# The head of the next sequence's Mamba block moved into the FFN, its convolution split over ACT and Pool, dt spread in larger packets

## The chip, the cores and the metric

One core of one Trainium2 chip runs the whole kernel in one launch. The metric is the device time of an execution in microseconds, the median over the timed runs. The five engines are called PE (TensorE), DVE (VectorE), ACT (ScalarE), Pool (GpSimd) and SP (SyncE, which here only issues DMAs).

## The reference

The reference is a two-layer decoder over 16 independent sequences (batch) of 256 tokens with 256 features, all in float32. Six sublayers follow each other, each as `x = layernorm(x + sublayer(x))`:

```
xz = x @ W_in (256 -> 1024);  xin, z = split(xz)
xc = silu(causal_depthwise_conv(xin, 4 taps) + conv_b)          # 512 channels
dt_low, Bm, Cm = split(xc @ W_xproj, [64, 16, 16])
dt = softplus(dt_low @ W_dt + b_dt)
h_t = exp(dt_t * A) * h_(t-1) + dt_t * B_t * xc_t               # 16 states a channel, 256 steps
y = (sum_n h*C + xc*Dp) * silu(z);  out = y @ W_out
```

That is the first, Mamba. Then come a latent cross-attention (16 heads of 16, 64 chosen keys a query), an FFN with quantised activations and ternary weights (256 -> 1024 -> 256, GELU, two inner norms), a self-attention (16 heads of 16), a cross-attention (16 heads of 64) and a mixture of eight experts with six chosen, plus a shared one. Mamba, latent attention and FFN are layer 0; the other three are layer 1.

## The kernel before

Each engine has one program of its own, and semaphores order them. A sequence is a unit of work: its 256 tokens are handled as 2 x 128 rows, or as 256 columns when channels lie on partitions. Inside, the work is two streams. Stream x is `mamba`, `latent` and `ffn` of a sequence; stream y is `self_attention`, `cross_attention` and `moe` of the sequence before. On each engine, each stream is a generator that yields between pieces, and `merged` (L58) interleaves the two by a written-out string: `ORDER` (L41) says for each engine how many pieces stream x is ahead at the start and then the turns of one period ("x9 y3 x1 ..."), repeated for every sequence. An engine works strictly in that order; a piece that waits holds all behind it. The state of a sequence's x goes from x to y through `X.x_ready`, whose third count comes from `ffn_end` (L1546): the last residual add and norm.

`mamba` of a sequence, before: PE projects 8 tiles of 128 channels (`projected`, L494) into four PSUM banks. ACT copies the first half of each bank into `xin` (L980) and writes the last tap's product with the bias into `conv` (L983); DVE adds the other three taps with twelve fused steps (L1383). ACT applies SiLU (L999, L1003). PE makes the low-rank dt (L516) and C rows (L519), the full dt in two halves (L543), the B rows (L549). DVE adds dt's bias (L1395), ACT computes the parts of the softplus (L1015 to L1018), DVE puts them together and multiplies by xc (L1406 to L1413). In between, a table of how often each key was chosen is counted by one-hot matmuls (L471), turned (L480) and made into a mask.

The state recurrence then runs in `UNITS` = 32 units. A unit has 8 channels x 16 states on the 128 partitions and 2 x 256 columns. Its dt rows and dt*x rows must be repeated 16 times over the partitions: SP stores them to a buffer in DRAM, `rows_of_dt` (L323), and reads them back with a repeating pattern, `spread_rows` (L325), one DMA of 256 KB for each unit and each of dt and dt*x, into four slots each. Per unit ACT writes exp(dt*A) to PSUM (L1028), DVE multiplies dt*x by B (L1432) and runs the scan along the columns (L1449), Pool multiplies by C (L1227), and PE sums over states, four units at a time (L561). ACT may be at most two units ahead of the scan; the spread of unit k waits for the decay, or the product, of unit k - 4. `gate` (L1418) and the output projection (L569) end the block.

`region_x`, one SBUF tensor of 11,792 words a partition, is carved into overlapping tiles that stages use in turn. xc, zs, conv, xin and the softplus tiles share its words with the FFN's tiles (`fh`, `qb`, `qT`), so the head of a `mamba` can begin to write only when the FFN before it is through.

In `ffn`, DVE's steps (norm, quantisation, L1527, one-hots L1351) alternate with small bf16 matmuls. In `moe`, PE makes gate and up groups of two tiles (L864), spreads the routing weights (L870) and does the down product (L925); ACT applies SiLU (L1189), DVE multiplies twice (L1646, L1650). ACT holds one set of functions at a time; `table` (L950) loads another when a piece needs it (L952).

Of the kernel before, what the change touches and what calls it, by code (L numbers as in the profile page):

```python
# [21 lines left out]
SLOTS = 4  # L22
# [70 lines left out]
X_STEPS = 70  # L93
END_STEPS = 5
DIGIT_STEPS = 8
Y_STEPS = 38
A_STEPS = 7
# [22 lines left out]
def build(nc, dram, out):  # L120

    ctx = ExitStack()
    with ctx:
# [45 lines left out]
        RX, RY = 11792, 9216  # L169
# [22 lines left out]
        PAD = T + TAPS - 1  # L192
        xc, zs, yT, csb = in_x(0, (M, T)), in_x(1024, (M, T)), in_x(2048, (M, T)), in_x(3072, (T,))
        conv = yT
        dtr = in_x(11536, (T,))
        xin = in_x(3328, (M, PAD))
        sp_l = in_x(3328, (M, T))
        sp_x, sp_e, sp_u = in_x(4364, (M, T)), in_x(5388, (M, T)), in_x(6412, (M, T))
# [3 lines left out]
        oh_hi, oh_lo = in_x(4608, (P, 32), BF16), in_x(10508, (P, 16), BF16)  # L202
        cnt = in_x(6656, (P, 16), BF16)
# [16 lines left out]
        scratch = nc.dram_tensor("rows_of_dt", (2, 2, P, M * T), F32)  # L220
# [16 lines left out]
        dt_exp = sem("dt_exp")  # L237
        digit_step, end_step = sem("digit_step"), sem("end_step")
        xz, xin_sb, conv_done, silu_x, silu_z = sem("xz"), sem("xin_sb"), sem("conv_done"), sem("silu_x"), sem("silu_z")
# [72 lines left out]
        att1 = Attention("self", 4, False, 1, VP1, nm1, in_y, 7424)  # L312
        att2 = Attention("cross", 4)

        block = ctx.enter_context(nc.Block())


        @block.sync
# [1477 lines left out]
```

## Time and profile before

| | |
|---|---|
| median of 3 timed runs | 3942.16 us (3936.2 to 3948.75) |
| the profiled execution | 3951.12 us, its span 3949.3 us |
| busy: PE, DVE, ACT, Pool | 3210.4 (81%), 3004.6 (76%), 1953.3 (49%), 650.5 (16%) |
| DMA | 470.84 MB, mean 119 GB/s |
| chain that ended last | PE 41%, DVE 34%, ACT 9%, issue 8%, DMA 6% |
| granted TensorE clock, mean | 0.933 |

A span is the time from the first to the last instruction of one profiled execution. Busy time of an engine counts its instructions' durations, overlaps once. The "chain that ended last" is followed back from the last instruction through whatever released each step. The program repeats one period for each sequence, so the tables below cut one steady period (1424.0 to 1657.8 us from the start) into stretches.

### The profile page before, as it was taken

How to read it: one execution, taken by the hardware profiler on the slowest of the kernel's cores; microseconds unless marked ns; L12 is line 12 of the kernel's file. 1: busy time of each engine (PE TensorE's matmuls, PEld its weight loads, DVE VectorE, ACT ScalarE, POOL GpSimd, SP SyncE). 2: the span in 40 equal slices, each digit the busy share in tenths (PEclk: the TensorE clock that was granted, in tenths of full speed). 3: DMA queues.
4: the chain of work that ended last, by engine and by line, in shares of the span. 5: the costliest groups of instructions: out<-in, count | busy, mean ns of one | idle time of the engine just before them, and what ended most of it. 6: DMA issues, size and time to landing. Idle time of an engine off the chain costs nothing.

```text
span 3949.3 us, 57618 instructions
## 1 busy us (share of the span) xinstructions
PE 3210.4 (81%) x21250; PEld 2199.1 (56%) x21250; DVE 3004.6 (76%) x6496; ACT 1953.3 (49%) x4513; POOL 650.5 (16%) x516
## 2 busy tenths in 40 slices
PE   2468988788797888978888897988879888887877
PEld 1245656556464655646556564655646565564655
DVE  5678796877878688796868879687887868778632
ACT  2336455564545546455554645555464554645422
POOL 0303030120303012040210304021030301204000
PEclk8679999999999989999999999989999998999987
DMA  6526171532716235181523517153361614427100
GB/s 213 131 56 174 50 197 63 157 119 89 203 50 184 77 123 153 54 238 49 155 95 116 171 50 225 52 159 99 96 196 50 197 63 146 130 74 215 55 31 16
DMA packets 205833, 470.84 MB, mean 119 GB/s; under 512 B 23856, under 2 KB 43952, under 8 KB 190832
## 3 DMA queue, kind: packets, MB, share of 16 engines
q1 hardware_dynamic: 205552, 467.17, 39.2%
q8 instruction: 167, 2.74, 0.3%
q14 instruction: 114, 0.93, 0.1%
HBM read 446.11 MB, written 20.97 MB: 118 GB/s over the span
## 4 chain that ended last, share of the span: by engine, by line
PE 41%; DVE 34%; ACT 9%; issue 8%; DMA 6%; SPq 1%; POOL 0%; DVEq 0%; ACTq 0%
DVE region_x L1449 7%; PE ps L864 6%; DMA region_x<-rows_of_dt 5%; DVE region_x L1432 5%; PE ps L633 4%; PE ps L824 3%; PE ps L810 3%; PE ps L497 3%; ACT region_y L1148 3%; PE ps L845 3%; PE ps L614 2%; DVE nm L1486 2%; PE ps L645 2%; DVE x_stats L1284 2%; PE ps L569 2%
## 5 line engine op out<-in xcount | busy, mean ns | idle before, releaser
L1227 POOL TENSOR_TENSOR region_x<-region_x 128x512 f32<-128x512 f32 x512 | 650.3, 1270 | 2982.6 <-DVE region_x L1449 2982.6
L1028 ACT ACTIVATE ps<-region_x,aneg 128x255 f32<-128x255 f32 x1024 | 443.1, 470 | 446.2 <-DVE region_x L1449 431.3
L1449 DVE TENSOR_TENSOR_SCAN region_x<-ps,region_x 128x512 f32<-128x512 f32 x512 | 622.9, 1217 | 16.0 <-ACT ps L1028 15.1
L1432 DVE TENSOR_TENSOR region_x<-region_x,ps 128x512 f32<-128x512 f32 x512 | 343.1, 671 | 49.2 <-DMA region_x<-rows_of_dt 46.2
L864 PE MATMUL ps<-xTy,wide 128*128 128x256 f32 x1280 | 307.1, 395 | 0.0
L1148 ACT ACTIVATE region_y<-ps,rmax 128x256 f32<-128x256 f32 x512 | 235.7, 500 | 140.9 <-DVE rmax L1591 140.9
L1499 DVE SCALAR_TENSOR_TENSOR region_x<-region_x,cntk 128x512 f32<-128x512 f32 x256 | 167.0, 689 | 156.2 <-ACT region_x L1066 156.2
L864 PEld LDWEIGHTS ps<-xTy,wide 128*128 128x128 f32 x1280 | 244.5, 196 | 42.3 <-issue 10.1
L561 PE MATMUL ps<-region_x,sely 128*32 128x512 f32 x1024 | 157.5, 691 | 121.6 <-POOL region_x L1227 121.3
L614 PE MATMUL ps<-region_y 64*128 64x256 f32 x1024 | 176.9, 485 | 91.5 <-DVE VP L1572 37.4
L633 PE MATMUL ps<-region_y 64*128 64x256 f32 x1024 | 173.1, 464 | 95.9 <-ACT region_y L1066 49.5
L1591 DVE TENSOR_REDUCE rmax<-ps 128x4 f32<-128x1024 f32 x128 | 153.2, 1218 | 111.2 <-PE ps L791 109.7
L1482 DVE CUSTOM_DVE_ANT_0 region_x<-ps,mask 128x256 f32<-128x256 f32 x512 | 184.7, 420 | 40.1 <-issue 40.1
L925 PE MATMUL ps<-down,region_y 128*128 128x256 f32 x640 | 183.4, 454 | 37.2 <-DVE region_y L1650 37.2
L1164 ACT ACTIVATE region_y<-ps 128x512 f32<-128x512 f32 x256 | 140.6, 597 | 142.1 <-PE ps L813 142.1
L633 PEld LDWEIGHTS ps<-region_y 64*128 64x128 f32 x1024 | 103.0, 217 | 190.9 <-ACT region_y L1066 131.3
L614 PEld LDWEIGHTS ps<-region_y 64*128 64x128 f32 x1024 | 113.4, 236 | 155.0 <-DVE nm L1486 60.6
L1066 ACT ACTIVATE region_x<-ps 128x512 f32<-128x512 f32 x256 | 141.2, 605 | 86.6 <-PE ps L633 86.6
L925 PEld LDWEIGHTS ps<-down,region_y 128*128 128x128 f32 x640 | 146.0, 233 | 64.9 <-issue 38.7
L791 PE MATMUL ps<-region_y 64*128 64x256 f32 x1024 | 138.7, 406 | 41.7 <-DVE region_y L1586 24.6
L1066 ACT ACTIVATE region_y<-ps 128x512 f32<-128x512 f32 x256 | 138.3, 593 | 52.9 <-PE ps L633 52.0
L810 PE MATMUL ps<-region_y 64*128 64x256 f32 x1024 | 156.5, 397 | 8.9 <-ACT shiftT L1157 7.6
(246 smaller groups left out, 6491.9 us busy)
## 6 DMA issues: line engine op xcount, KB each, us to landing
region_x<-rows_of_dt SPq DMA_DIRECT2D x1024, 256.0 KB, 5.3
wide<-in_wgate SPq DMA_DIRECT2D x16, 1280.0 KB, 8.4
wide<-in_wup SPq DMA_DIRECT2D x16, 1280.0 KB, 11.0
down<-in_wmoe SPq DMA_DIRECT2D x16, 1280.0 KB, 5.6
wide<-in_wq SPq DMA_DIRECT2D x16, 1024.0 KB, 4.8
wide<-in_wk SPq DMA_DIRECT2D x16, 1024.0 KB, 6.9
wide<-in_wv SPq DMA_DIRECT2D x16, 1024.0 KB, 8.9
down<-in_wo SPq DMA_DIRECT2D x16, 1024.0 KB, 7.8
```

Source lines behind the costliest of these rows:

```text
L614: last = mm(ps[:, b + j, qt * T:(qt + 1) * T], a.QT[r, t, qt * P:(qt + 1) * P], a.KT[u % 2][r, t, :], start=True, stop=True)
L633: last = mm(ps[:, a.sT_bank(n + j), kt * T:(kt + 1) * T], a.KT[e][r, t, kt * P:(kt + 1) * P], a.QT[r, t, :], start=True, stop=True)
L810: mm(ps[:, b, kt * T:(kt + 1) * T], KT2[r, t, kt * P:(kt + 1) * P], QT2[r, t, :], start=True, stop=False)
L864: last = mm(bank(b)[:, j, :], w[:, k, f * P:(f + 1) * P], xTy[:, k, :], start=(k == 0), stop=(k == KD - 1))
L925: last = mm(bank(7)[:, tt, :], mhT[:, f, tt * P:(tt + 1) * P], wmoe[:, f, :], start=(n == 0), stop=(n == KM - 1))
L1028: last = f(ps[:, 1 + 2 * (k % 2), m * T + 1:(m + 1) * T], dt_rep[k % SLOTS][:, m, 1:T], ACT.Exp, scale=aneg[:, k, m:m + 1])
L1066: f(a.PT[:, n % 8].rearrange("p k q -> p (k q)"), ps[:, a.sT_bank(n), :], ACT.Exp).then_inc(a.probs, 1)
L1148: last = f(junk2[:, 4 * (u % 2) + 2 * qt + g], ps[:, a.pair_bank(u) + g, qt * T:(qt + 1) * T], ACT.Exp, bias=rmax[:, qt, g, u:u + 1], accu ...
L1227: nc.gpsimd.tensor_tensor(hbuf[k % HSLOTS], hbuf[k % HSLOTS], csb.unsqueeze(1).to_broadcast([P, 2, T]), ALU.mult).then_inc(hc_ready, 1)
L1432: tt_(hbuf[k % HSLOTS], dtx_rep[k % SLOTS], ps[:, 2, 0:T].unsqueeze(1).to_broadcast([P, 2, T]), ALU.mult).then_inc(dbx, 1)
L1449: nc.vector.tensor_tensor_scan(flat(hbuf[k % HSLOTS]), ps[:, 1 + 2 * (k % 2), :], flat(hbuf[k % HSLOTS]), 0.0, ALU.mult, ALU.add).then_inc ...
L1482: last = nc.vector.tensor_tensor_reduce(a.junk[:, 4 * (u % 2) + 2 * qt + j], ps[:, b + j, qt * T:(qt + 1) * T], mask[:, qt, :], -1.0, HUGE ...
```

## The change

Six things change together.

1. The head of the next sequence's Mamba (in-projection, convolution, gates, low rank, C rows, dt, B rows, turned counts) is issued inside `ffn` of the present one. Only the joining of dt's second half, the masks and the counts by key stay in `mamba`. The head of sequence 0 runs ahead of both streams.
2. `region_x` grows by 5,376 words, in which xc, zs, conv, the taps, C and the softplus tiles lie apart from the FFN's.
3. The convolution: ACT makes all four products from PSUM (three of them into `taps`, shifted), Pool adds them, three serial sums for each half.
4. dt's bias is added by ACT instead of DVE.
5. The store to DRAM lays two groups of channels next to each other, and one DMA spreads two units: 512 KB, 4,096 bytes a partition and packet, three slots of two units.
6. All four turn strings are new; also some PSUM banks in the FFN, and a smaller scratch for software DMA. With the new turns the y stream of a sequence starts eight units into the next sequence's scan, and the second part of `moe` lies at the scan's beginning.

The core of the diff:

```
-SLOTS = 4
+COUPLES = 3
...
-        RX, RY = 11792, 9216
+        EARLY = 11792
+        RX, RY = EARLY + 5376, 9216
...
-        dt_rep = [in_x(7436 + 512 * s, (2, T)) for s in range(SLOTS)]
-        dtx_rep = [in_x(9484 + 512 * s, (2, T)) for s in range(SLOTS)]
+        dt_rep = [in_x(at_word, (2, 2, T)) for at_word in (7436, 8460, 0)]
+        dtx_rep = [in_x(at_word, (2, 2, T)) for at_word in (9484, 10508, 0 + 1024)]
...
-        scratch = nc.dram_tensor("rows_of_dt", (2, 2, P, M * T), F32)
+        scratch = nc.dram_tensor("rows_of_dt", (2, 2, 2, 32, 4, 2 * T), F32)
...
+            def spread_rows(i, what, d, dst):
+                rows = scratch[i % 2, what, d // 8, 8 * (d % 8 // 2):8 * (d % 8 // 2) + 8, 2 * (d % 2):2 * (d % 2) + 2]
+                return sp.dma_start(dst.rearrange("p k m t -> p (k m t)"),
+                                    rows.rearrange("r j f -> r (j f)").unsqueeze(0).to_broadcast([NS, 8, 4 * T]))
...
+                for d in range(UNITS // 2):
+                    slot = couple(i, d)[0]
...
+                    if d >= COUPLES:
+                        sp.wait_ge(decay_ready, at(i, UNITS, 2 * (d - COUPLES) + 2))
+                    spread_rows(i, 0, d, dt_rep[slot]).then_inc(rep_dt[slot], 16)
...
# PE, in ffn
+                        projected(i + 1, n)            # two pieces, at the start
...
+                    projected(i + 1, 2)                # after the FFN's first product
+                    projected(i + 1, 3)
+                    yield from low_rank(i + 1)         # low rank, C rows, dt
+                    pe.wait_ge(silu_z, i + 2)
                     yield from counted(i + 1, 0, 2)
...
+                    yield from b_rows(i + 1)           # after the FFN's second product
+                    yield from counted(i + 1, 2, 4)
+                    yield from counts_turned(i + 1)
...
+            def conv_products(i, half):
+                act.wait_ge(xz, at(i, 4, half + 1))
+                if half:
+                    act.wait_ge(conv_sum, at(i, 6, 3))
+                for j in range(2):
+                    m = 2 * half + j
+                    f(conv[:, m, :], bank(half)[:, j, :], ACT.Identity, bias=W["convb"][:, m:m + 1],
+                      scale=W["convw"][:, m, TAPS - 1:TAPS])
+                    for k in range(TAPS - 1):
+                        late = TAPS - 1 - k
+                        last = f(taps[k][:, j, late:T], bank(half)[:, j, 0:T - late], ACT.Copy,
+                                 scale=W["convw"][:, m, k:k + 1])
+                last.then_inc(taps_sb, 1)
...
+            def conv_sums(i):                          # Pool, after the 32 products of a sequence
+                for half in range(2):
+                    pool.wait_ge(taps_sb, at(i, 2, half + 1))
+                    part = conv[:, 2 * half:2 * half + 2, :]
+                    for k in range(TAPS - 1):
+                        if k:
+                            pool.wait_ge(conv_sum, at(i, 6, 3 * half + k))
+                        nc.gpsimd.tensor_tensor(part, part, taps[k], ALU.add).then_inc(conv_sum, 1)
...
# DVE, mamba
-                            ins = stt(conv[:, m, :], xin[:, m, k:k + T], W["convw"][:, m, k:k + 1], conv[:, m, :],
-                                      ALU.mult, ALU.add)
...
+                yield from dt_half(dt_steps, i, 1)
```

The order of the pieces around the handover, as the new strings give it (x7 is stream x of sequence 7, y5 stream y of sequence 5, and so on):

```
ACT: ... x6 cnt3 | x7 rstd5 | y5 gate0 | x7 decay0 | y5 gate1 wT | x7 decay1 | y5 gate2 | x7 decay2 | y5 gate3 | x7 decay3 | y5 gate4 | x7 decay4..7 ...
SP:  x6 rows, choices+xT | x7 store0 | y5 ctx | x7 store0' | y5 wide_moe | x7 spreads 0, 1, store1, spread 2 | y5 wmoe | x7 spreads 3, 4 | y5 wide_cross | x7 spread 5 | y5 wo2, out | x7 spread 6 ...
```

## Rows read from the trace of the kernel before

**Rows 1.** By stretch: us, busy of PE, PEld, DVE, ACT, Pool; clock, DMA, GB/s.

```profile
1424.00:1657.80 233.80, 198.82 (x1336) 136.95 (x1332) 186.66 (x405) 121.90 (x283) 40.65 (x32) 0.95 0.40 123
1424.00:1452.50 28.50, 26.13 (x128) 20.00 (x124) 20.16 (x52) 16.96 (x32) 0.00 (x0) 0.94 0.27 83
1452.50:1536.50 84.00, 64.29 (x387) 37.19 (x387) 79.42 (x106) 44.12 (x105) 40.65 (x32) 0.92 0.82 236
1536.50:1603.30 66.80, 62.52 (x490) 43.82 (x489) 37.27 (x126) 40.04 (x112) 0.00 (x0) 1.00 0.07 28
1603.30:1657.80 54.50, 45.88 (x335) 35.94 (x333) 49.80 (x123) 20.79 (x35) 0.00 (x0) 0.94 0.24 89
```

**Rows 2.** The head in two parts, then two DVE groups of it (count, busy us, mean ns).

```profile
1424.00:1438.50 14.50, 14.50 (x80) 10.66 (x76) 10.50 (x33) 10.84 (x20) 0.00 (x0) 1.00 0.00 1
1438.50:1452.50 14.00, 11.63 (x51) 9.34 (x50) 9.66 (x19) 6.12 (x12) 0.00 (x0) 0.88 0.55 167
...
L1383 DVE SCALAR_TENSOR_TENSOR region_x<-region_x,convw 128x256 f32<-128x256 f32 x12 | 5.3, 483 | 0.8 <-ACT region_x L983 0.6
L1395 DVE TENSOR_SCALAR region_x<-ps,bdt 128x256 f32<-128x256 f32 x4 | 1.7, 479 | 2.1 <-PE ps L543 2.1
```

**Rows 3.** Instruction groups of the scan stretch, DVE.

```profile
L1449 DVE TENSOR_TENSOR_SCAN region_x<-ps,region_x 128x512 f32<-128x512 f32 x32 | 39.0, 1217 | 0.9 <-ACT ps L1028 0.8
L1432 DVE TENSOR_TENSOR region_x<-region_x,ps 128x512 f32<-128x512 f32 x32 | 21.4, 671 | 1.9 <-DMA region_x<-rows_of_dt 1.7
```

**Rows 4.** Instruction groups of the FFN stretch, PE and DVE.

```profile
L864 PE MATMUL ps<-xTy,wide 128*128 128x256 f32 x80 | 18.5, 385 | 0.0
L925 PE MATMUL ps<-down,region_y 128*128 128x256 f32 x40 | 11.6, 458 | 2.3 <-DVE region_y L1650 2.3
...
L1646 DVE TENSOR_TENSOR region_y<-region_y,ps 128x512 f32<-128x512 f32 x4 | 2.7, 684 | 0.2 <-PE ps L864 0.2
```

**Rows 5.** Instruction groups of the scan stretch that the new order takes out.

```profile
L765 PE MATMUL ps<-wide,ctxT 128*128 128x512 f32 x16 | 7.1, 599 | 0.0
L779 PE MATMUL ps<-xTy,wide 128*128 128x256 f32 x32 | 7.4, 386 | 0.7 <-ACT xTy L969 0.7
L791 PE MATMUL ps<-region_y 64*128 64x256 f32 x24 | 3.1, 393 | 2.3 <-DVE region_y L1586 1.5 <-ACT region_y L1148 0.9
...
L1586 DVE TENSOR_SCALAR region_y<-ps 128x512 f32<-128x512 f32 x4 | 2.6, 681 | 0.0
L1591 DVE TENSOR_REDUCE rmax<-ps 128x4 f32<-128x1024 f32 x2 | 2.4, 1223 | 0.1
```

**Rows 6.** ACT's table loads of the period, and one in order of time.

```profile
L952 ACT ACT_TABLE_LOAD x7 | 9.0, 1283 | 0.1
...
1425.94 1.28 ACT L952 ACT_TABLE_LOAD   x1
1427.23 0.60 ACT L980 ACTIVATE region_x<-ps 128x512 f32<-128x512 f32 x1
```

**Rows 7.** Order of time, Pool and DVE (start us, us, what).

```profile
1510.89 1.26 POOL L1227 TENSOR_TENSOR region_x<-region_x 128x512 f32<-128x512 f32 x1 [0.43 <-DVE region_x L1449]
...
1510.90 1.28 DVE L1297 SCALAR_TENSOR_TENSOR y_nt<-y_nt,y_rstd 128x2 f32<-128x2 f32 x1
```

**Rows 8.** Spreads, then expert weights, by stretch; and one row of the DMA issues.

```profile
1480.00:1490.00 10.00, 8.22 (x80) 3.75 (x72) 7.87 (x10) 8.85 (x21) 5.86 (x5) 1.00 1.02 258
1530.50:1541.00 10.50, 8.63 (x56) 5.95 (x56) 7.35 (x10) 5.55 (x24) 2.47 (x2) 1.00 0.99 407
...
wide<-in_wup SPq DMA_DIRECT2D x16, 1280.0 KB, 11.0
```

**Rows 9.** Order of time, PE: first transposes of three y streams.

```profile
269.88 0.66 PE L459 MATMUL ps<-ident,xh 128*128 128x128 f32 x4
...
3539.45 0.66 PE L459 MATMUL ps<-ident,xh 128*128 128x128 f32 x4
...
3759.80 1.09 PE L459 MATMUL ps<-ident,xh 128*128 128x128 f32 x4 [4.13 <-DVE xh L1303]
```

More of the change, by code:

```diff
@@ new lines, in projected, with low_rank @@
+            def projected(i, n):
+                for m in (2 * n, 2 * n + 1):
+                    for k in range(KD):
+                        last = mm(bank(n)[:, m % 2, :], W["win"][:, k, m * P:(m + 1) * P],
+                                  xTx[:, k, :], start=(k == 0), stop=(k == KD - 1))
+                last.then_inc(xz, 1)
+            def low_rank(i):
+                yield
+                for k in range(M):
+                    pe.wait_ge(silu_x, at(i, 2, k // 2 + 1))
+                    last = mm(ps[0:RANK, 0, 0:T], W["wxd"][:, k, :], xc[:, k, :], start=(k == 0), stop=(k == M - 1))
+                last.then_inc(xdbl, 1)
+                yield
+                for k in range(M):
+                    last = mm(ps[:, 1, 0:T], W["wc"][:, k, :], xc[:, k, :], start=(k == 0), stop=(k == M - 1))
+                last.then_inc(xdbl, 1)
@@ L679, in ffn @@
             def ffn(i):
+                more = i + 1 < B
+                for n in range(2):
+                    yield
+                    if more:
+                        if n == 0:
+                            pe.wait_ge(xT_loaded, at(i + 1, 16, 16))
+                            pe.wait_ge(X.sum_read, at(i, 3, 2))
+                        projected(i + 1, n)
                 psb = ps[:, 3, :].bitcast(BF16).rearrange("p (a b) -> p a b", b=T)
@@ L931, in all_first @@
                     pass
+                pe.wait_ge(xT_loaded, 16)
+                for n in range(3):
+                    projected(0, n)
+                pe.wait_ge(cnt_sb, 4)
+                projected(0, 3)
+                for piece in (low_rank, b_rows, counts_turned):
+                    for _ in piece(0):
+                        pass
                 for i in range(B):
@@ L1199, in all_first @@
                     count_copy(0, r)
+                for half in range(2):
+                    conv_products(0, half)
+                gates(0)
+                for half in range(2):
+                    conv_half(0, half)
+                dt_rank(0)
+                c_copy(0)
+                for half in range(2):
+                    softplus_parts(0, half)
                 before = None
@@ L1222, in _ @@
         def _(pool):
+            def conv_sums(i):
+                for half in range(2):
+                    pool.wait_ge(taps_sb, at(i, 2, half + 1))
[4 more added lines that the diff above has]
+                        nc.gpsimd.tensor_tensor(part, part, taps[k], ALU.add).then_inc(conv_sum, 1)
+            conv_sums(0)
             for i in range(B):
@@ L1389, in mamba @@
-                yield
-                next(before, None)
-                for half in range(2):
-                    yield
-                    v.wait_ge(dt_ps, at(i, 2, half + 1))
-                    for m in (2 * half, 2 * half + 1):
-                        last = ts(sp_x[:, m, :], bank(half)[:, m % 2, :], W["bdt"][:, m:m + 1], None, ALU.add)
-                    last.then_inc(dt_x, 1)
+                next(before, None)
+                yield from dt_half(dt_steps, i, 1)
+                dt_steps.close()
@@ L1454, in mamba @@
                 gate(1)
+                for k in range(TAPS - 1):
+                    nc.vector.memset(taps[k][:, :, 0:TAPS - 1 - k], 0.0)
                 v.wait_ge(x_loaded, at(i, 16, 16))
@@ L1538, in ffn @@
                 yield from quantised(i, c, fh, FF, 3)
+                if i + 1 < B:
+                    yield from dt_half(next_steps, i + 1, 0)
+                else:
+                    yield from [None] * 2
                 for r in (2, 3):
@@ L1664, in all_first @@
                 before = iter(())
+                steps = Chain(v, dt_step, 0, DT_STEPS)
+                for _ in dt_half(steps, 0, 0):
+                    pass
                 for i in range(B):
                     c = Chain(v, vx_step, i, X_STEPS)
-                    yield from mamba(i, c, before)
+                    yield from mamba(i, c, before, steps)
                     if i == 0:
@@ L1670, in all_first @@
                     yield from latent(i, c)
-                    yield from ffn(i, c)
+                    steps = Chain(v, dt_step, i + 1, DT_STEPS)
+                    yield from ffn(i, c, steps)
                     c.close()
```

325 lines of the change are left out of this document (147 added, 178 removed), and 17 rows, old and new, of the table ORDER.

## The prediction

> **What bounds the kernel now.** I read the busy shares by stretch first, then the instruction groups of each stretch, then the waits and the DMA issues. Two streams run interleaved: x (Mamba, latent attention, FFN of one sequence) and y (self-attention, cross-attention, experts of the sequence before). One steady period, from one x stream's FFN end to the next, is the first row of [rows 1]: 233.8 us, PE busy 198.8, DVE 186.7, ACT 121.9. Neither big engine fills it; each stretch has its own limit.
>
> - Head, 28.5 us: PE 26.1. Its first 14.5 us (in-projection to turned counts) are PE without a gap [rows 2]; the scan can't start before it ends.
> - Scan, 84.0 us: DVE 79.4, PE only 64.3.
> - Latent and cross scores, 66.8 us: PE 62.5.
> - FFN beside the experts, 54.5 us: DVE 49.8, PE 45.9.
>
> The limits add up to 26.1 + 79.4 + 62.5 + 49.8 = 217.8, so 16.0 us a period are stalls and handovers. What is wasted is PE under the scan, 84.0 - 64.3 = 19.7 us, because there DVE alone sets the pace: each of 32 units costs a scan of 1217 ns and a product of 671 ns [rows 3].
>
> **The change, part by part, for one period.**
>
> Taken off DVE: twelve convolution steps, 5.3 us, and four bias adds, 1.7 us [rows 2]: 7.0 us. DVE's total becomes 186.7 - 7.0 = 179.7.
>
> PE's total stays 198.8: the same matmuls, moved. The head's 14.5 us go between the latent attention's end and the FFN's end, where the previous order had the experts. In exchange the whole second part of the experts and the self-attention's projections come under the scan. I walked the new turn strings, piece by piece, to see what lies beside what:
>
> - Into the scan stretch, PE: projections and turns of the self-attention, the head's second part, 11.6 [rows 2]; six of the ten gate or up groups, 0.6 x 18.5 = 11.1; the experts' down product, 11.6; the weights' spreading, an estimate of 1.5 (eight matmuls at no more than the down product's 11.6 / 40 would be 2.3) [rows 4]. Together 35.8.
> - Out of it, PE: cross values 7.1, cross queries 7.4, first scores 3.1, and one key group, 1.85 like a gate group [rows 4, 5]: 19.4.
> - PE there: 64.3 + 35.8 - 19.4 = 80.7. DVE there: 79.4, plus eight expert products of 0.68 (four stand in [rows 4], four more cost the same) = 5.4, plus the experts' norm, an estimate of 3.1 (one wide add of 0.68, four steps on 256 columns at 0.48 as in [rows 2], and 0.5 of tiny ones), plus the self queries, four such steps, 1.9, minus cross queries 2.6 and two maxima 2.4 [rows 5]: 84.8.
> - The rest of the period: PE 198.8 - 80.7 = 118.1; DVE 179.7 - 84.8 = 94.9.
>
> The limits are now 84.8 (DVE) and 118.1 (PE), sum 202.9 against 217.8. I keep the 16.0 us of stalls, since the dependency chains inside latent attention, FFN and self-attention are untouched, and add 5 for what is new:
>
> *ACT.* It gets sixteen products on 256 columns where it had two copies and four scaled steps, and the four bias adds: fourteen more, at most 0.6 each like the wide copy of [rows 6], 0.4 in a row, so +6 us. It also alternates: the new order runs gate 0, decay 0, gate 1, decay 1 and so on to gate 4, and each needs another table set. Seven loads of 1283 ns a period [rows 6] become about fourteen, +9 us. ACT has 112 us idle, so the sum costs nothing there; but in five units the chain gate, decay, next gate is 0.6 + 1.0 + 2 x 1.28 = 4.2 us long (the two decays at the same rate as the copy), beside PE's 2 x 1.85 = 3.7 for an expert pair. Lower bound 0, upper bound 5 x (4.2 - 1.9) = 11.5 us, if those units wait for nothing else. I take 3, near zero, because PE sets the pace of that stage anyway.
>
> A page says more. The Trainium skill, page "ScalarE: Activation LUTs", section "What ACT_TABLE_LOAD costs", gives each switch a drain of about the same length again, 2.66 us in all. Here the copy behind a load starts at 1427.23, 1.29 us after the load's start [rows 6], so the trace disagrees; by the page the seven extra loads would cost 19 us of ACT instead of 9, and the exposed part would double, a period of about 227.
>
> *Pool.* Six sums of 128x512, serial in threes; the same form of instruction takes 1.27 us, so 7.6 us in the FFN stretch, where Pool had been idle. The first product half waits for nothing, the second for Pool's first three sums, since the tap buffers are shared; both have some 15 us before the low-rank product needs them, so this latency is hidden. What isn't: at 1510.90 a DVE step on two columns took 1.28 us, as long as the Pool product of 512 columns that started 0.01 us before it [rows 7]. Bounds: 0 if DVE's neighbours read PSUM (as scans and products do, which run beside Pool unharmed), 7.6 if each sum holds DVE once. I take 2.
>
> That observation has a name: the Trainium skill, "SBUF — State Buffer", section "SBUF: two separate sides", calls the pair of ports that DVE and GpSimd share an exclusive lock, held for a whole instruction when DVE has two SBUF inputs. By that rule, which the row bears out, the FFN's two-input steps would pay in full; it is the first rival below.
>
> *DMA.* Spreads move the same bytes in half as many packets. With 2,048-byte packets the engines are saturated at 258 GB/s; loading expert weights they reach 407 [rows 8]. The new rate lies between these. At best the 4.6 us go that DVE idles under the scan [rows 1]; at worst a spread of twice the size lands later than the lead allows, which is now about five units of 1.9 us where it was four: from -4.6 to about +2. I take 0. The weight loads are the third rival.
>
> *Late things.* Once the head is gone, the next late item before the scan is the second half of dt (DVE about 3.1 us) and the masks; both lie beside expert matmuls.
>
> Period: 202.9 + 16.0 + 5 = 223.9, that is -9.9.
>
> **The whole run.** y streams start at 269.9 (first), 3539.5 (15th) and 3759.8 (16th) [rows 9]: 14 periods of 233.5, a last one of 220.3 without a next sequence, and 189.5 to the end. After: the first y stream must wait for the x stream's FFN with the head inside, and for eight units of scan. I put +19 on it (16 for the units at two microseconds each, 9 for Pool's serial sums and the next dt, less the 6 or so of head that now hides in the lone FFN), so 289. The last period drops the head (14.5) and the table switching: 223.9 - 20 = 203.9. Sum: 289 + 14 x 223.9 + 203.9 + 189.5 = 3817. The profiled execution took 3951.1 for a span of 3949.3, and the median of the timed runs is 3942.2, 9 below it: 3817 + 2 - 9 = 3810.
>
> **The rivals.** One microsecond a period is 15 in the run.
>
> 1. *The port between Pool and DVE costs in full.* 7.6 instead of 2: 3810 + 15 x 5.6 = 3894. For: the row above, and that the sums fall beside the FFN's norms, which read two SBUF tensors. Against: DVE isn't the limit there (94.9 of some 129). Chance 0.14.
> 2. *The long PE stretch fills badly.* PE was busy 45.9 of 54.5 in the FFN stretch, 84%; if that share holds for all the rest, 118.1 / 0.84 = 140.6 instead of about 129, less 3 that the scan stretch would keep of its stalls: +8.5 a period, 3937. For: FFN is a serial chain on DVE. Against: cross scores now lie beside it, and with such filler PE reached 94%. Chance 0.12, half of it no change.
> 3. *Slower: the SP queue.* The loads of the expert gates and ups now stand behind the first dt store, and those of the down product and the next cross weights between spreads. At 407 GB/s these 2.56, 1.28 and 3.07 MB take 6.4 + 3.2 + 7.7 = 17.3 us, formerly issued long before use; the second of the expert loads landed 11.0 us after its issue [rows 8]. Spreads behind them in the queue come late, DVE waits. All exposed: 3810 + 15 x 17.3 = 4070. It decides once more than 8.8 of the 17.3 are exposed. For: SP blocks on each load's own wait. Against: by my walk some 10 us of PE and DVE work (two count blocks, the state rows, the residual norm, the router) stand between that issue and the first gate product, so 3 us are exposed there at most. Chance 0.12.
> 4. *Better.* The stalls shrink too (DVE's 4.6 us under the scan go, and with them some of PE's time at a lower granted clock, 0.92 there against 1.00 after it [rows 1]): -7 a period, 3705. Chance 0.13.
>
> **How the numbers follow.** The forecast (3750 to 3875) has 0.49. No change means within 0.3%, 12 us, about what a measurement of this kernel can tell. Faster: 0.49 + 0.14 + 0.13 + half of rival 2 = 0.82, less 0.02 for the forecast's own tail; one of these goes to the same, 0.06 + 0.01 = 0.07, one to slower, 0.12 + 0.01 = 0.13. The range leaves out rival 3, half of rival 2 and the tail of rival 4: 3710 to 3935.
>
> **What would show it.** Right: a steady period near 224; no gap-free PE head before the scan; PE above 85% under the scan; conv steps gone from DVE and Pool at 48.3 us a period; fourteen table loads a period. Wrong: DVE idle in the first scan units on "DMA region_x<-rows_of_dt" or PE idle before the first gate group on weights (rival 3); DVE rows of the FFN above their old means (rival 1); PE below 88% from latent attention to FFN end (rival 2).

## The result: slower, by 7.9%

The changed kernel takes 4259.3 us (median of 4 runs, 4251.3 to 4261.2), the kernel before 3945.5 (4 runs): ratio 1.079, 95% interval 1.076 to 1.082. The forecast was 3810 us, with a range up to 3935. The profiled execution has a span of 4249.5 us.

The page of the kernel after, its engines and the rows that answer to [rows 6, 8] (the last three lines are DMA issues: count, KB each, median us to landing):

```profile
PE 3276.5 (77%) x21234; PEld 2233.4 (53%) x21250; DVE 2970.2 (70%) x6275; ACT 2141.2 (50%) x4802; POOL 775.0 (18%) x612
DMA packets 131337, 470.81 MB, mean 111 GB/s; under 512 B 14896, under 2 KB 34992, under 8 KB 116336
...
L968 ACT ACT_TABLE_LOAD x209 | 268.1, 1283 | 4.4 <-PEq L1849 0.7
...
region_x<-rows_of_dt SPq DMA_DIRECT2D x512, 512.0 KB, 8.6
...
wide<-in_wup SPq DMA_DIRECT2D x16, 1280.0 KB, 17.1
down<-in_wmoe SPq DMA_DIRECT2D x16, 1280.0 KB, 15.9
```

The work is what was forecast: the steps of the convolution have left DVE, Pool has six sums more a period, 14 table loads stand in a period. What is different is when DMAs land: the load of the experts' up weights (wup) takes 17.1 us where it took 11.0 [rows 8].

The y streams, in order of time on PE, as in [rows 9]:

```profile
310.23 0.69 PE L466 MATMUL ps<-ident,xh 128*128 128x128 f32 x2
...
3833.92 0.55 PE L466 MATMUL ps<-ident,xh 128*128 128x128 f32 x3
...
4059.66 0.55 PE L466 MATMUL ps<-ident,xh 128*128 128x128 f32 x3 [0.78 <-DVE xh L1384]
```

A steady period is (3833.92 - 310.23) / 14 = 251.7 us; it was 233.5, and 223.9 was forecast. The other terms: first y start 310.2 for 289, last period 225.7 for 203.9, 189.8 to the end for 189.5. So of the 432 us by which the sum (3817) missed the span, 14 x 27.8 = 389 lie in the steady periods. This section and the next look for them there; "period" always means this quotient of a profiled execution.

One period, from a first scan to the next, in three parts cut at places that both orders have: first to last scan; on to the end of latent attention; on to the next first scan. Columns as in [rows 1]. The kernel before, cut this way:

```profile
1216.15:1295.45 79.30, 60.42 (x356) 35.08 (x358) 73.35 (x94) 40.60 (x92) 39.38 (x31) 0.92 0.84 221
1295.45:1371.19 75.74, 68.75 (x530) 47.36 (x526) 43.85 (x142) 43.06 (x123) 1.26 (x1) 1.00 0.17 64
1371.19:1455.63 84.44, 72.49 (x447) 56.16 (x446) 69.61 (x169) 38.35 (x67) 0.00 (x0) 0.91 0.24 83
```

The kernel after; behind it the stretch around the scan's start in which DMA is full, and 10 us of it in which only spreads are in flight:

```profile
1291.82:1384.06 92.24, 68.27 (x403) 43.26 (x402) 78.09 (x104) 49.61 (x102) 39.23 (x31) 0.92 0.79 205
1384.06:1466.73 82.67, 71.29 (x458) 50.13 (x458) 45.59 (x148) 39.04 (x116) 1.46 (x2) 0.99 0.06 21
1466.73:1544.17 77.44, 62.50 (x472) 44.71 (x472) 60.99 (x140) 46.10 (x84) 7.78 (x6) 0.89 0.35 107
...
1279.00:1350.00 71.00, 57.50 (x290) 40.77 (x288) 51.55 (x78) 34.89 (x62) 20.36 (x16) 0.92 0.88 245
...
1336.00:1346.00 10.00, 6.29 (x36) 4.40 (x38) 9.89 (x13) 2.62 (x6) 3.81 (x3) 0.83 1.03 243
```

The period shown of the kernel before is its longest, 239.5 us. Over the 13 steady periods of each, the three parts are on the mean 77.1, 75.8 and 80.8 us before and 92.5, 81.5 and 77.5 us after, so the differences are read from these.

Read three things here. The last part got only 3 us shorter on the mean: DVE (61.0) and PE (62.5) both sit idle for 15 to 16 us of it. The scan got 15 us longer, with only 4.5 more of DVE work (means of 73.1 and 77.6). And DMA is as good as full from 13 us before the scan to 58 us into it (0.88), while it is nearly idle, 21 GB/s, for the 83 us after. Spreads alone fill the engines at 243 GB/s with packets of 4,096 bytes, where it was 258 with 2,048 [rows 8], in a window that also holds a load of the next x: the larger packets bought no rate.

The waits of the kernel after (total us, times, longest); for the first row the kernel before had 46.2:

```profile
DVE region_x L1485 <- DMA region_x<-rows_of_dt: 145.3, 86, 8.2
DVE cntq L1433 <- PE ps L487: 107.0, 14, 9.0
...
PE ps L872 <- DMA wide<-in_wup: 102.0, 14, 8.0
...
DVE xh L1384 <- PE ps L933: 51.6, 16, 9.1
```

And the place of the third row in one period, PE in order of time:

```profile
1278.33 6.30 PE L872 MATMUL ps<-xTy,wide 128*128 128x256 f32 x16 [7.42 <-DMA wide<-in_wup]
1284.56 1.17 PE L487 MATMUL ps<-identb,region_x 32*128 32x32 bf16 x16
1285.66 3.72 PE L872 MATMUL ps<-xTy,wide 128*128 128x256 f32 x16
```

The first expert group waits 7.4 us for its weights and then runs at a lower clock, 6.30 us for what takes 3.72 right after (the granted clock is 0.72 on the mean of 1273 to 1291.8, so for somewhat over half of that time it is at the lower of its two levels, 1.2 of 2.4 GHz). The counts that DVE needs (L487) stand behind it on PE, so DVE waits as well: the second row of the waits.

### The profile page after: what moved, and what is told of

Read it like the earlier page. It is cut to its first block, busy times and chain, and to the rows that moved or that the text cites. A ratio compares the mean times of both kernels' runs of the same rounds, so it can differ in the third digit from the quotient of the medians.

```text
span 4249.5 us, 57375 instructions
## 1 busy us (share of the span) xinstructions
PE 3276.5 (77%) x21234; PEld 2233.4 (53%) x21250; DVE 2970.2 (70%) x6275; ACT 2141.2 (50%) x4802; POOL 775.0 (18%) x612
## 4 chain that ended last, share of the span: by engine, by line
PE 37%; DVE 23%; ACT 15%; DMA 15%; issue 7%; SPq 2%; POOL 1%; DVEq 0%; POOLq 0%; ACTq 0%
DMA region_x<-rows_of_dt 6%; DMA wide<-in_wup 6%; PE ps L601 4%; PE ps L872 4%; DVE region_x L1502 4%; PE ps L933 3%; ACT region_y L1195 3%; PE ps L620 3%; DMA out_x<-xh 3%; PE ps L787 2%; PE ps L773 2%; DVE region_x L1485 2%; ACT ps L1053 2%; PE ps L502 2%; DVE nm L1541 2%
## 5 line engine op out<-in xcount | busy, mean ns | idle before, releaser
L1294 POOL TENSOR_TENSOR region_x<-region_x 128x512 f32<-128x512 f32 x512 | 650.7, 1272 | 1737.3 <-DVE region_x L1502 1737.3
L872 PE MATMUL ps<-xTy,wide 128*128 128x256 f32 x1280 | 330.1, 416 | 102.0 <-DMA wide<-in_wup 102.0
L1287 POOL TENSOR_TENSOR region_x<-region_x 128x512 f32<-128x512 f32 x96 | 124.1, 1293 | 1390.4 <-ACT region_x L1002 1385.4
L872 PEld LDWEIGHTS ps<-xTy,wide 128*128 128x128 f32 x1280 | 260.3, 209 | 152.4 <-DMA wide<-in_wup 103.4
L601 PE MATMUL ps<-region_y 64*128 64x256 f32 x1024 | 179.9, 494 | 118.0 <-DVE VP L1631 65.4
L620 PE MATMUL ps<-region_y 64*128 64x256 f32 x1024 | 185.1, 491 | 98.8 <-ACT region_y L1091 59.6
L1195 ACT ACTIVATE region_y<-ps,rmax 128x256 f32<-128x256 f32 x512 | 237.9, 496 | 16.6 <-DVE rmax L1650 14.5
L601 PEld LDWEIGHTS ps<-region_y 64*128 64x128 f32 x1024 | 116.3, 240 | 197.2 <-DVE VP L1631 86.5
L620 PEld LDWEIGHTS ps<-region_y 64*128 64x128 f32 x1024 | 109.5, 231 | 186.8 <-ACT region_y L1091 134.5
L799 PE MATMUL ps<-region_y 64*128 64x256 f32 x1024 | 143.4, 399 | 75.7 <-ACT region_y L1195 61.7
L1211 ACT ACTIVATE region_y<-ps 128x512 f32<-128x512 f32 x256 | 141.6, 594 | 107.1 <-PE ps L821 106.8
L1384 DVE TENSOR_TENSOR xh<-ps,xh 128x512 f32<-128x512 f32 x80 | 55.2, 690 | 199.0 <-PE ps L662 71.0
L818 PE MATMUL ps<-region_y 64*128 64x256 f32 x1024 | 165.7, 415 | 16.9 <-ACT region_y L1211 15.0
## 6 DMA issues: line engine op xcount, KB each, us to landing
wide<-in_wup SPq DMA_DIRECT2D x16, 1280.0 KB, 17.1
wide<-in_wv SPq DMA_DIRECT2D x16, 1024.0 KB, 13.8
```

The costliest lines, as they stand in the source:

```text
L601: last = mm(ps[:, b + j, qt * T:(qt + 1) * T], a.QT[r, t, qt * P:(qt + 1) * P], a.KT[u % 2][r, t, :], start=True, stop=True)
L620: last = mm(ps[:, a.sT_bank(n + j), kt * T:(kt + 1) * T], a.KT[e][r, t, kt * P:(kt + 1) * P], a.QT[r, t, :], start=True, stop=True)
L818: mm(ps[:, b, kt * T:(kt + 1) * T], KT2[r, t, kt * P:(kt + 1) * P], QT2[r, t, :], start=True, stop=False)
L872: last = mm(bank(b)[:, j, :], w[:, k, f * P:(f + 1) * P], xTy[:, k, :], start=(k == 0), stop=(k == KD - 1))
L1195: last = f(junk2[:, 4 * (u % 2) + 2 * qt + g], ps[:, a.pair_bank(u) + g, qt * T:(qt + 1) * T], ACT.Exp, bias=rmax[:, qt, g, u:u + 1], accu ...
L1294: nc.gpsimd.tensor_tensor(hbuf[k % HSLOTS], hbuf[k % HSLOTS], csb.unsqueeze(1).to_broadcast([P, 2, T]), ALU.mult).then_inc(hc_ready, 1)
```

## The experiments

Each ran beside the kernel before on the same chip; from chip to chip the median of the kernel before differs by at most 6 us (3941 to 3947). e4 and e5 leave work out and only show what it costs. The table has the median, the ratio to the kernel before, the period, and DVE's wait for spreads summed over the run.

| run | us | ratio, 95% interval | period | DVE on spreads |
|---|---|---|---|---|
| before | 3945 | 1 | 233.5 | 46 |
| after | 4259 | 1.079 (1.076 to 1.082) | 251.7 | 145 |
| e1_wide_early | 4201 | 1.064 (1.062 to 1.066) | 247.3 | 223 |
| e2_out_late | 4232 | 1.071 (1.069 to 1.074) | 250.5 | 263 |
| e3_small_packets | 4225 | 1.070 (1.068 to 1.072) | 250.1 | 136 |
| e4_pool_tiny | 4140 | 1.049 (1.047 to 1.051) | 243.7 | 268 |
| e5_cross_tiny | 4106 | 1.041 (1.039 to 1.043) | 241.3 | 121 |
| e6_before_cross_late | 4001 | 1.015 (1.013 to 1.018) | 237.1 | 85 |
| e7_fewer_tables | 4184 | 1.062 (1.060 to 1.063) | 247.4 | 129 |
| e8_sums_on_dve | 4181 | 1.060 (1.058 to 1.062) | 246.7 | 224 |
| e9_moe_early | 4148 | 1.053 (1.050 to 1.056) | 243.9 | 147 |
| e10_loads_apart | 4143 | 1.051 (1.048 to 1.054) | 243.5 | 121 |
| e11_loads_last | 4058 | 1.028 (1.026 to 1.030) | 237.9 | 60 |
| e12_all_mended | 4110 | 1.041 (1.038 to 1.043) | 241.9 | 60 |
| e13_sums_dve_only | 4041 | 1.024 (1.021 to 1.026) | 236.8 | 58 |
| e14_small_packets_clean | 4061 | 1.029 (1.026 to 1.033) | 238.4 | 59 |

**First four: which of the suspects, queue order, packets, Pool.**

```
e1   sp order: -"x14 y1 x1 y1 x8 ..."  +"x13 y2 x10 ..."          (ctx, wgate, wup ahead of store 0)
e2   e1, and  -"... x2 y2 x10"  +"... x4 y2 x8"                  (wo2, output store behind couple 6)
```

> SyncE's order alone is changed: the context rows and the two wide expert loads (wgate, wup) are issued before the first dt store instead of behind it. Theory A (the queue order is the loss): the wait of PE for wup at the first gate group (7.3 us, 14 times) goes, and the slow clock after it (the group ran 6.3 instead of 3.7 us), so 7 to 10 us in each of some 15 periods: 4259 becomes 4110 to 4155 us. Theory B (DMA bandwidth is the loss, the order only says who waits): the spreads and stores wait instead, and no more than 3 us per period come back: 4215 us or more. Theory C (Pool sums holding DVE up, and PE's own new stretch, are the loss): within 15 us of 4259.

> As the run before, and the loads of wo2 and the output store are issued behind the spreads of couple 6 instead of ahead of them. Theory A: DVE's three spread waits at units 9 to 13 (3.79, 2.75 and 2.25 us) shrink, and as DVE sets the scan 4 to 8 us per period more come back: 60 to 120 us below the run before. Theory B: the spreads are late because DMA is full, so the waits only move by a couple: less than 30 us below it.

e1 came between the theories. PE's wait for wup is gone from the trace and the last part of the period falls from 77 to 70 us, but DVE's spread waits grow from 145 to 223 us: more than half of what PE gave back was waited for again under the scan. e2 is worse than e1 by 31 us, against theory A: the loads that it moved now stood ahead of other couples. Both say that the queue has no room where these loads stand.

```
e3   one transfer of [128, 2 units] per couple -> two of [128, 1 unit], semaphore counts 32
```

> The kernel after with each spread of a couple as two transfers with packets of 2,048 bytes, as before, in the same order and at the same place in SyncE's queue. Theory A: the packets don't matter, the landing is set by what stands ahead: 4259 with at most 25 us either way (32 more issues per period on SyncE may cost some). Theory D (the larger transfers are late because both units of a couple land together): the first unit lands earlier, DVE's and ACT's waits for rows_of_dt (145 and 70 us) at least halve, and the time falls by 60 us or more.

34 us faster, 9 beyond the bound of theory A and far from the 60 of D; DVE's wait for spreads hardly changed (136), that for wup fell by 12. So the packets' size had some part beside the large loads; through what is not shown, for the two waits make up 21 of the 34 us. e14 below repeats it with these loads moved.

```
e4   e2, and  -tensor_tensor(part, part, taps[k], add)  +tensor_tensor(part[:, :, 0:8], ..., taps[k][:, :, 0:8], add)
```

> As the run with wo2 and the output store late, but the three Pool sums of the convolution work on 8 of the 256 columns only (most of the sums are left out; instructions, waits and order are the same). If GpSimd's hold on the port costs what the lengthened DVE steps show (0.9 to 0.16, 1.98 to 0.91 and so on, 5 to 6 us a period, plus up to 3 us of latency of the sums before silu), the time falls by 60 to 120 us against that run; if DVE isn't what sets the FFN's end (PE is), by less than 25 us.

92 us less than e2 by the medians, about 6 a period. By the profiled executions it is 6.8, but that of e2 is its slowest, 16 us above its median. DVE's steps under a Pool sum in the kernel after:

```profile
1220.65 0.91 DVE L1368 SCALAR_TENSOR_TENSOR x_nt<-x_mv,x_rstd 128x2 f32<-128x2 f32 x1 [1.18 <-ACT x_rstd L981]
...
1221.79 1.12 DVE L1370 SCALAR_TENSOR_TENSOR x_rstd<-x_nt,x_rstd 128x2 f32<-128x2 f32 x1
1222.94 1.98 DVE L1377 SCALAR_TENSOR_TENSOR region_x<-region_x,x_rstd,ln1b 128x256 f32<-128x256 f32 x2
...
1228.04 1.23 DVE L1403 TENSOR_SCALAR region_x<-region_x 128x256 bf16<-128x256 f32 x1
1229.20 0.21 DVE L1409 CAST region_x<-idx 128x128 f32<-128x128 int32 x1
1229.45 1.18 DVE L1410 TENSOR_SCALAR region_x<-region_x 128x128 f32<-128x128 f32 x1
1230.66 1.38 DVE L1411 TENSOR_TENSOR region_x<-region_x 128x128 f32<-128x128 f32 x1
```

and the same steps with the sums cut to 8 columns, then the last part of the period in that run:

```profile
1439.58 0.16 DVE L1368 SCALAR_TENSOR_TENSOR x_nt<-x_mv,x_rstd 128x2 f32<-128x2 f32 x1 [1.18 <-ACT x_rstd L981]
...
1439.97 0.16 DVE L1370 SCALAR_TENSOR_TENSOR x_rstd<-x_nt,x_rstd 128x2 f32<-128x2 f32 x1
1440.16 0.88 DVE L1377 SCALAR_TENSOR_TENSOR region_x<-region_x,x_rstd,ln1b 128x256 f32<-128x256 f32 x2
...
1444.17 0.29 DVE L1403 TENSOR_SCALAR region_x<-region_x 128x256 bf16<-128x256 f32 x1
...
1444.63 0.23 DVE L1410 TENSOR_SCALAR region_x<-region_x 128x128 f32<-128x128 f32 x1
1444.89 0.29 DVE L1411 TENSOR_TENSOR region_x<-region_x 128x128 f32<-128x128 f32 x1
...
1433.44:1496.73 63.29, 59.86 (x473) 43.45 (x472) 55.33 (x139) 45.95 (x84) 2.39 (x6) 0.97 0.24 65
```

The part is 63.3 us long with DVE busy 55.3; in e2 it is 70.1 with 61.1. Six sums of 1.27 us, 7.6 in all, take 5.8 us of DVE. With that gone the part is 6.8 us shorter, so once the weights are there DVE's chain sets its length, though PE is as busy (61.7 us in e2, 59.9 in e4).

**Second four: bytes, the same fault in the old kernel, table loads, the sums' place.**

```
e5   e1, and load_wide_cross() -> load_wide_cross(32)             (32 of 1,024 columns after the first time)
e6   before, sp order: -"x2 y3 x1 y1 x17 y1 x5 ..."  +"x2 y3 x17 y1 x1 y1 x5 ..."
e7   e1, act order: -"y1 x1 y2 x1 y1 x1 y1 x1 y1 x4 y1"  +"y1 x1 y3 x2 y2 x5 y1"
e8   e1, conv_sums() off Pool; the same six adds in DVE's stream, behind the norm and behind the digits
```

> As e1_wide_early, but the three cross-attention weights (3.07 MB a period) are loaded in full only once; later loads bring 32 of 1,024 columns (most of the transfer is left out; issues and waits stay). Theory B, as the first runs have changed it (the queue is full from about 13 us before the first scan to 58 us after it, so weights that the new order reloads beside the spreads cost DVE their transfer time): DVE's 14.0 us of spread waits a period fall to 5 or less, and 9 to 11 us a period come back: 4201 becomes 4035 to 4070. Theory A (the order in the queue alone matters, and DMA has room): less than 3 us a period, 4155 or more.

> The kernel before, with one thing of the change: SyncE issues the cross-attention weights behind the spreads of unit 6's predecessors, so among the spreads, instead of ahead of the first dt store. Theory B: the same loss appears in the old kernel, 3.07 MB at 250 to 400 GB/s = 8 to 12 us a period less 2 to 4 of slack: 3946 becomes 4030 to 4110. Theory A: the weights are needed only after 16 units, the buffers are four units ahead, nothing waits: within 30 us of 3946.

e5 gives 95 us back and halves DVE's spread waits, from 223 to 121: the bytes count, though less than theory B had it, 6.0 us a period for loads of 3.15 MB (the 3.07 MB of the expectations counts the page's KB, which are 1,024 bytes, as 1,000). e6 shows the loss in the old kernel: nothing but the place of the cross weights in SyncE's queue, with their use far off, costs 59 us (3.6 a period). That is less than the 84 to 164 expected and well clear of nothing, and PE never waits for these weights in it. Its one row of the waits, the kernel before with the cross weights among the spreads:

```profile
DVE region_x L1432 <- DMA region_x<-rows_of_dt: 84.8, 86, 5.4
```

The bytes are not all. SyncE issues in its written order, and a wait of its own holds all behind it. Two such waits of the kernel after, one for the experts' down product before wo2 is loaded, one for the output store to land before the next x is loaded:

```profile
SPq L421 <- PE ps L933: 105.1, 15, 9.3
SPq L336 <- DMA out_x<-xh: 92.3, 14, 8.7
```

In the kernel before the first happens once (14.6 us) and the second is not among the waits. e5 shows what such waits can do with the bytes out of the way: SyncE in order of time, and a stretch of the same trace.

```profile
1263.34 1.20 SPq L332 DMA_DIRECT2D region_x<-rows_of_dt  x2
1271.36 0.33 SPq L421 DMA_DIRECT2D down<-in_wo  x1
1275.08 0.40 SPq L424 DMA_DIRECT2D out_x<-xh  x1
1275.54 1.17 SPq L332 DMA_DIRECT2D region_x<-rows_of_dt  x2
...
1268.00:1272.00 4.00, 3.42 (x20) 2.69 (x22) 3.00 (x4) 0.00 (x0) 2.73 (x3) 1.00 0.40 118
```

DMA falls to 0.40 while the next couple isn't issued, and DVE waits 1.54 us for spreads at 1283.54. By couple, counted from 0, DVE's waits over the run fall from 87 us in e1 to 1 in e5 at couple 5, the first behind the cross weights, but only from 34 to 23 and from 32 to 31 at couples 6 and 7, which stand behind wo2, the store and the next x. In the kernel after DMA stays full (1.02 and 1.03) through the same two waits of SyncE, so there its waits and the bytes can't be told apart; no run takes SyncE's waits out alone.

> As e1_wide_early, but ACT runs gate 0, decay 0, gates 1 and 2, decays 1 and 2, gates 3 and 4, decays 3 and on: 9 instead of 13 table loads a period. If the switching sets the pace of the five expert pairs, 2 to 5 us a period come back: 4125 to 4170. If PE's pairs or the spreads set it: within 20 us of 4201, or somewhat slower because decays 1 and 3 come later.

> As e1_wide_early, with the six convolution sums on DVE instead of Pool: DVE gets 6 x 0.69 = 4.1 us of work and loses what Pool's sums cost it (5.8 us a period between e2_out_late and e4_pool_tiny, if that was the port and not the serial latency of Pool's sums). Port theory: 1 to 2.5 us a period faster, 4165 to 4190. If the 92 us of e4_pool_tiny were latency instead, DVE's own 2.1 us for three sums instead of 4.1 halves that and the FFN stretch falls by 3 us or more: 4155 or less. If neither: 4201 + 60.

e7: 17 us less, within the bound of "no effect"; DVE waits 94 us less for spreads but 60 for ACT's later decays and 79 for the experts' product, which were 27 and 26 in e1. e8: 20 us less, 0.6 us a period and an earlier first stream, the low end of what the port theory allowed and not the latency theory's 45. DVE trades 5.8 us of blocking for 4.1 of adds.

**Then: where the loads can stand.** The first spreads land some 10 us before the first scan, so a load ahead of them should be free; a couple has under 1 us of queue to spare (two transfers of 524,288 bytes at 243 to 258 GB/s are 4.1 to 4.3 us, and two units of scan took 79.3 / 16 = 5.0 in the kernel before).

```
e9   sp order "x13 y2 x2 y1 x12 y1 x2 y2 x10"                     (wmoe ahead of couple 0)
e10  sp order (78, "y2 x2 y1 x12 y1 x6 y1 x6 y1 x8 y2 x5"): wmoe as e9; wk2, wv2, wq2 apart, each with its own
     semaphore, behind couples 4, 7, 10; output store, wo2 and next x behind couple 14
e11  e10, these three behind couple 15: "... x10 y2 x3"
```

> As e1_wide_early, and the load of the experts' down product (1.28 MB) is issued ahead of the first spread instead of behind the third couple. Queue theory: the first spreads land 10 us before the first scan and have that much to give, so nothing is late there, and the 3.5 us of queue that stood between couples 2 and 3 leave the stretch in which the queue is full: DVE's 14.0 us of spread waits fall by 3 to 4, 4201 becomes 4140 to 4160. If the waits come from the couples' own round trip (issue when two units have been read, landing 8 to 10 us later whatever stands ahead): less than 15 us.

> As e9_moe_early, and nothing else large stands in the queue at once: the three cross weights go one at a time behind couples 4, 7 and 10, output store, wo2 and the next x behind couple 14. The bytes of a period are the same. Queue theory: the 2.5 MB of store, wo2 and x leave the full stretch and no couple meets more than 1 MB ahead of it: DVE's spread waits fall to 4 to 7 us, 4085 to 4125. Rate theory (couples take 4.1 us of queue for 5.2 us of scan, and 3.07 MB more fill the rest): the waits move to later couples, not below 9 us: 4140 or more.

> As e10_loads_apart, but output store, wo2 and the next x come behind the last couple (15) instead of behind couple 14, where the last couple waited 5.1 us for them. Queue theory: those 5 us a period go, DVE's spread waits fall from 7.2 to 2 to 3 us, 4143 becomes 4060 to 4085. Rate theory: they move to another couple, 4125 or more. In both it stays above the kernel before (3943), because DVE's work beside the scan (84.6 instead of 79.4 us) and the latent stretch (81 to 84 instead of 76 us) are as in the kernel after.

e9 fell by 53 us, as the queue theory said. e10 didn't: the waits at couples 5 to 7 went, save one of 1.65 us, and one of 5.07 us came near the end of the scan. The last couple was issued only at 1338.61: before it SyncE had issued the store (1329.19) and wo2, then stood some 8 us until the store had landed to load the next x (1338.19). From then to the end of DVE's wait DMA isn't even full (0.76, then 0.63), so here SyncE's wait counts more than the bytes. The row in e10, DVE in order of time:

```profile
1346.45 0.69 DVE L1495 TENSOR_TENSOR region_x<-region_x,ps 128x512 f32<-128x512 f32 x1 [5.07 <-DMA region_x<-rows_of_dt]
```

e11 moved these three by one couple and the 84 us came. The scan stretch of e11, and its waits:

```profile
1248.71:1337.03 88.32, 66.52 (x402) 43.07 (x401) 77.96 (x104) 49.55 (x102) 39.21 (x31) 0.93 0.82 215
```

```profile
DVE region_x L1495 <- DMA region_x<-rows_of_dt: 59.6, 53, 7.7
DVE xh L1394 <- PE ps L943: 51.6, 16, 9.1
```

All bytes are as in the kernel after and every engine's instructions too; 201 us of 314 are gone by SyncE's order alone (and two more semaphores). The granted clock is back with it, 0.931 on the mean of the execution where the kernel after has 0.908.

**Last: do the gains add, and the packets once more.**

> As e11_loads_last, with the convolution sums on DVE (alone it gave 20 us) and ACT's order with fewer table loads (alone 17 us). If the three losses are independent: 30 to 40 us below e11_loads_last, so 4025 to 4050. If the fewer table loads only helped because the spreads were late, 15 to 20 us below it, or a little more than nothing when decays 1 and 3 now come late: 4045 to 4070. Beating the kernel before is not expected.

```
e12  e11 + e8 + e7        e13  e11 + e8        e14  e11 + e3
```

e12 was wrong in both of its versions: 51 us slower than e11. Two rows of its scan, DVE in order of time:

```profile
1263.47 1.22 DVE L1506 TENSOR_TENSOR_SCAN region_x<-ps,region_x 128x512 f32<-128x512 f32 x1 [3.23 <-ACT ps L1063]
1277.77 0.69 DVE L1388 TENSOR_TENSOR xh<-ps,xh 128x512 f32<-128x512 f32 x1 [4.24 <-PE ps L943]
```

In e11 these two waits are 0.97 and 2.39 us; over the whole run they are 59 and 79 us in e12, 27 and 52 in e11. With the spreads on time, the decays that ACT runs later, and the experts' product, are what DVE waits for.

> As e11_loads_last, with the convolution sums on DVE and ACT's order left as in the kernel after. If e12_all_mended lost its 51 us to the later decays (DVE waited 3.7 us for ACT and 4.3 us for the experts' product a period, where it had 1.4 and 2.4): the sums alone give what they gave before, 15 to 25 us, so 4033 to 4045. If the sums on DVE are what cost it: 4080 or more.

> As e11_loads_last, with each couple's spread as two transfers of 2,048-byte packets. In the kernel after this gave 34 us. If that gain was only that small packets let a large load behind or ahead of them interleave better, it is gone here, where nothing large stands in the queue at once: within 15 us of 4058. If the large packets themselves, or both units of a couple landing together, cost time: 4025 to 4040 again.

Both came as the first reading of each said. The sums on DVE give 17 us again, so e12's loss, 68 us against e13, is ACT's order with its four table loads less (10 instead of 14 a period). And with no large load beside the spreads the packets' size makes no difference (+3 us): e3's gain needed the large loads there. e13 is the fastest variant of the change, 2.4% slower than the kernel before.

## Why the prediction was wrong

Its steps, by where the 27.8 us a period between 223.9 and 251.7 are.

- **"DMA. I take 0", and rival 3 at 0.12.** This is the step that failed most: 13.8 us (251.7 to 237.9 in e11). The term had bounds of -4.6 to +2, worked out for the spreads alone. The rows to see it were there: the scan stretch at 0.82 DMA share, with bursts at 1.02, against 0.07 and 0.24 after it [rows 1, 8]. The old order loaded the experts' gate and up weights behind the last spread, and their down product's and the cross weights after the scan; the new one can't issue the cross weights before the experts' last up product, which now lies inside the scan. Rival 3 saw the queue, but asked how long each load would be waited for by its own user: 3 us at most for wup, measured 7.4, and 2.6 more at the lower clock. Its lead was right (some 10 us; wup was issued at 1261.11 and PE stood from 1270.9), its landing was not, 17.1 us for 11.0. What cost more was behind the loads in the queue: e1, which takes PE's wait away, gives 4.4 us a period, the places of the other loads (e1 to e11) 9.4. There each couple of spreads came late, by the bytes ahead of it and by SyncE's own waits, which the rival named ("SP blocks on each load's own wait") and didn't price. Even all of its 17.3 us would have left 10 of the 27.8.
- The Trainium skill, "SBUF — State Buffer", section "Can I just issue two DMAs to hit both halves?", says that all DMAs of a kernel land on the same 16 engines, and that two at once, measured there, serialize. The runs agree: e6 costs the old kernel 59 us though SBUF targets, semaphores and users of the cross weights and the spreads have nothing in common.
- **"Pool ... I take 2", rival 1.** Measured 6 to 6.8 in e4, 5.8 of it DVE's busy time: 4 to 5 us of the miss. "Against: DVE isn't the limit there" failed: with PE freed of its wait, DVE is busy for 61 of 70 us and its chain paces the FFN (e4). The step also counted only two-input operations; L1403 and L1410, with one SBUF input, took 1.23 and 1.18 us for 0.29 and 0.23. The Trainium skill, "SBUF — State Buffer", section "Who interferes with whom", counts tensor_scalar in a two-port mode among the operations that take the shared pair. The rows agree.
- **The limits, 202.9 instead of 217.8.** By the three-part cut above, the busiest engine of each part adds up to 73.1 + 68.8 + 69.6 = 211.5 us before and 77.6 + 69.9 + 62.1 = 209.6 after (means of 13 periods). So the limits fell by 2 us, not by 14.9. In part the sum was uneven: 217.8 took the larger engine of each stretch, 202.9 took PE alone for all that is behind the scan, and so dropped the 3.9 us by which DVE exceeded PE in the FFN stretch (49.8 and 45.9). For the rest, PE under the scan came to 68.8 us, not 80.7: it rose by 9, not by 16. Cross keys, values and queries all fell behind the last scan (the forecast had left most of the keys under it), and of the experts' 80 gate and up products 43 lie under it, not 48. PE waits for the cross weights in no run. The self-attention stands before them in its turns: its two rounds of score products idle for 15.7 us in the scan stretch, mostly on ACT and DVE; that this is what pushes the cross products out is likely but not shown. So the latent stretch, where PE is the busiest engine (71.3 of 82.7 us), got 6 us longer.

The three terms are 13.8, 4 to 5 and 13 us and overlap, for together they are more than 27.8; no run takes the third alone. An estimate of what the new order is worth by itself, e11's 237.9 less the whole of the lock, 6.8, is 231.1, or 2.4 us a period, close to the 2 by which the limits fell and far from 14.9.

PE's groups in the kernel after: the experts' in the scan stretch, then three in the latent stretch.

```profile
L872 PE MATMUL ps<-xTy,wide 128*128 128x256 f32 x43 | 10.0, 384 | 0.0
...
L763 PE MATMUL ps<-ctxT,wide 128*128 128x256 f32 x32 | 8.3, 413 | 0.0
...
L773 PE MATMUL ps<-wide,ctxT 128*128 128x512 f32 x16 | 7.7, 605 | 0.0
L787 PE MATMUL ps<-xTy,wide 128*128 128x256 f32 x32 | 7.6, 386 | 0.7 <-ACT xTy L985 0.7
```

- **ACT, +3 for table switching.** Fourteen loads a period as forecast. Its exposed cost was not isolated: the one way tried to take loads out cost more than it saved once spreads were on time (e12 against e13).
- **"First y start +19", "last period -20".** The first y stream started 40 us later, 21 more than forecast. Pool's sums have a part in it (313.6 us in e2, 305.9 in e4); the rest was not isolated. The last period was 22 us over its forecast only because the steady one was 28 over; against that one it was -26, better than forecast.

What was right: the instruction counts and their movement, Pool's 48.5 us and ACT's 14 loads a period, the signs to look for. The two that "would show it wrong" for rival 3 are both among the waits, DVE's not in the first scan units but mainly at couples 5 to 7.

What stays open is why e11 is still 4.4 us a period above the kernel before. Its three parts are 86.7, 81.7 and 69.4 us on the mean, for 77.1, 75.8 and 80.8: the last part gained 11.4 us, the other two lost 15.5, of which 4.4 is DVE's added work under the scan. Open too is whether keys and values could be brought back under the scan, since self- and cross-attention share their PSUM banks.

## What to carry to other kernels

When a change starts the next stage before the last one has freed its weights' buffer, list every DMA of the period with its bytes against the stretch in which its buffer is free and the stretch in which it is needed; a load that lands long before its use still delays whatever is queued behind it, and in a stretch that runs near DMA's rate most of that delay can be paid. The same holds for what the issuing engine itself waits for before a load. Price a DMA by its neighbours in the queue, not by its own user. And a gain found beside one loss (e7, 17 us) can turn into a loss (68 us) when the other is gone, so the pieces are measured again on the mended kernel.

## What the hardware showed that was not expected

- Spreads (one DRAM row to 16 partitions) fill the DMA engines at 243 GB/s with packets of 4,096 bytes and about 258 with 2,048, weights at 407 [rows 8]; with the large loads out of the way the number of packets, halved, changed nothing (e14, 4061 against 4058).
- With large loads in the queue the packets did matter: with 2,048-byte spreads the wait for wup fell from 102 to 90 us and the run by 34.
- After an idle of 7.4 us PE's granted clock was low enough that one expert group took 6.30 us instead of 3.72, so this wait cost a third more than its length.
- SyncE stood some 8 us for its own output store to land before it issued the last couple of e10; DVE then waited 5.07 us for that couple, with DMA at 0.63 to 0.76.
